# The last attention tile of a two-layer patch transformer: banks, projections and masked keys in another order

## The chip, the cores and the metric

One core of a Trainium2 chip runs the whole program. The metric is the device time of one execution in microseconds, the median of several runs. Engines are TensorE (PE in the profile, PEld for its weight loads), VectorE (DVE), ScalarE (ACT), GpSimd (POOL) and SyncE (SP, which only issues transfers here). All numbers are float32. PSUM, into which TensorE writes, has eight banks, numbered 0 to 7.

## The reference, cut to what matters

64 images give 49 patch tokens each, 3,136 rows of 192. There are two layers, each with a norm behind the residual:

```python
h = tok(x)                                   # (64, 49, 192)
h = layernorm(h + attention(h))              # causal, 12 heads of 16, relative positions
h = layernorm(h + attention2(h))             # qkv = h @ Wqkv.T + bqkv + routed low-rank delta
# attention2: softmax(q k^T * 0.25) v, then out @ Wproj.T + bproj
```

The change touches the end of the second layer alone: scores, softmax, weighting of the values, out-projection, residual and norm of the last tokens.

## The kernel before

The work is cut in two ways. **Tiles** of two images (98 tokens, `T`) carry the attention: 32 tiles in each layer. **Blocks** of 128 tokens carry the projections and norms: 25 blocks, 0 to 24, the last of 64 tokens. A hand-written order (`CHAINS`) gives each attention tile a slot; slots 0 to 63 hold the 64 tiles, `LAST` is 63, and the loops of every engine run over the slots to `SLOTS` = 67. Lists such as `OUT2` (out-projection of the second layer) and `QKV2` say in which slot a block is served. Each engine has its own program, and semaphores order them; an engine takes its instructions strictly as written.

In a slot n the steps are these. TensorE transposes the probabilities of the tile of slot n-1 (`transpose_probs`, L592, twice three transposes into banks 2 and 3), multiplies them with its values (`weigh_values`, L605, into bank 2) and computes the scores of slot n+1 (`scores`, L555, banks 0 and 1, but 4 and 5 for the last tile, whose scores come one slot early, in slot 62). VectorE finds the maximum, subtracts it, and behind the exponent sums, inverts and scales. ScalarE takes the exponent, copies the transposed probabilities to SBUF (`take_pt`, L824) and copies the weighted values y (`take_y`, L831). The wait on `yt_ready` at the head of `transpose_probs` keeps bank 2 until y of the tile before is out.

Scores need masked keys, a block-diagonal copy of k that GpSimd makes (`block_diagonal`, L420, L434). Weighting needs block-diagonal values (`vbd`), placed by small transfers on SyncE's queue (`place_values`, L379, L385) once the block's value rows are in SBUF (`take_v`, L822). A transfer of an output block (L398) goes on the same queue.

A finished block goes through `out_project` (L618, matmuls L623 and L624, bank 6), `add_residual` (L995, reads bank 6), `ln_stats`, `ln_aggregate`, `inverse_deviation` on ScalarE (L858) and `normalise` on GpSimd (L440: a shift, L445, and a scaling, L448). Its residual buffers are two, the output buffers `o_sb` three.

Near the end `keep_busy` (L661) issues matmuls of the identity into bank 7 whose result nobody reads: 21 calls in slots 63 to 66 (5, then 3, in slot 63; 2, 4 and 3 in slot 64; 2 in each of 65 and 66). Each call of one float32 matmul appears as two MATMUL rows.

The last five blocks, 20 to 24, are projected in slots 61, 63, 64, 65 and 66. Tile 31 (the last, slot 63) lies in blocks 23 and 24. In slot 61 GpSimd does the norm of block 19 first and then the masked keys of the last tile.

Of the kernel before, what the change touches and what calls it, by code (L numbers as in the profile page):

```python
# [30 lines left out]
RING = 6 * T  # L31
LEAD = 8
XS = 5
OS = 3
VR = 6
VB = 4
SCALE = 0.25
# [107 lines left out]
routers = by_slot(ROUTED)  # L145
qkv2s = by_slot(QKV2)

OUT2 = [n + 2 + (n + 2 in [m + 2 for m in DONE1] + [len(CHAINS) - 2]) for n in DONE2]
out2 = by_slot(OUT2)
norm2 = by_slot([n + (n < len(CHAINS)) for n in OUT2])  # L150

# [21 lines left out]
def score_bank(n):  # L173

    return 4 if n == LAST else 0


def moves(t):
# [33 lines left out]
def build(nc, x, tok_w, w1a_in, w1b_in, add1_in, const_in, p1_in, lora_in, w2_in, b2_in, p2_in, out):  # L212
    with ExitStack() as ctx:
# [40 lines left out]
        class Layer:  # L254
            def __init__(self, n):
                if n == 1:
                    self.q, self.k, self.mask, self.scale = qk1[0:64], qk1[64:128], kmask[64:128], SCALE
                else:
                    self.q = sb(f"q{n}", [64, 3, RING])
                    self.k = sb(f"k{n}", [64, 3, RING])  # L260
                    self.mask, self.scale = kmask[0:64], 1.0
                self.kbd = [sb(f"kbd{n}_{u}", [64, 2, 3, T]) for u in range(2)]
                self.vrow = [sb(f"vrow{n}_{u}", [128, E]) for u in range(VR)]
                self.vbd = [sb(f"vbd{n}_{u}", [PP, 2, E]) for u in range(VB)]
                self.res = [sb(f"res{n}_{u}", [128, E]) for u in range(2)]
                self.st = sb(f"st{n}", [128, 6])
                self.pad = sb(f"pad{n}", [1, 1])
                self.mv = sb(f"mv{n}", [128, BLOCKS, 2])
                self.lnv = sb(f"lnv{n}", [128, BLOCKS])
                self.rstd = sb(f"rstd{n}", [128, BLOCKS])  # L270
                self.shift = sb(f"shift{n}", [128, BLOCKS])
                self.qk_done = sem(f"qk_done{n}")
                self.qk_ready = sem(f"qk_ready{n}")
                self.kbd_ready = sem(f"kbd_ready{n}")
                self.v_done = sem(f"v_done{n}")
                self.v_rows = sem(f"v_rows{n}")
                self.v_ready = [sem(f"v_ready{n}_{u}") for u in range(VB)]
# [126 lines left out]
        def _(pool):  # L404
# [35 lines left out]
            def normalise(L, b, to):  # L440
                nonlocal upper
                k = tokens(b)
                pool.wait_ge(*moved_k)
                pool.wait_ge(L.rstd_ready, b + 1)
                nc.gpsimd.tensor_scalar(L.shift[0:k, b:b + 1], L.mv[0:k, b, 0:1], L.rstd[0:k, b:b + 1], -1.0,  # L445
                                        ALU.mult, ALU.mult).then_inc(L.shift_ready, 1)
                pool.wait_ge(L.shift_ready, b + 1)
                nc.gpsimd.tensor_scalar(to, L.res[b % 2][0:k], L.rstd[0:k, b:b + 1], L.shift[0:k, b:b + 1],  # L448
                                        ALU.mult, ALU.add).then_inc(L.ln_ready, 1)
                upper = L.ln_ready, b + 1  # L450

# [14 lines left out]
                    bias_values(b)  # L466
            for n in range(SLOTS):

                layer, t = attention(n + 2)
                known = bool(layer and (QKV1 if layer == 1 else QKV2)[block_of(t)] < n)  # L470
                if known:
                    block_diagonal(n + 2)
                for b in out1(n):
                    normalise(L1, b, h[0:tokens(b), b, :])
                for b in norm2(n):
                    if b >= OS:
                        pool.wait_ge(out_stored[b % OS], 16 * (b // OS))
                    normalise(L2, b, o_sb[b % OS][0:tokens(b)])
                if not known:
                    block_diagonal(n + 2)  # L480
                for b in turns(n):
                    bias_values(b)

        @block.tensor
        def _(pe):
# [104 lines left out]

            def transpose_probs(n, free):
                pf = probs[n % 2][:].rearrange("p h j -> p (h j)")  # L592
                if n > 0:
                    pe.wait_ge(yt_ready, n)
                if free:
                    pe.wait_ge(*free)
# [1 line left out]
                for half in range(2):  # L598
                    for g in range(3):
                        k = (3 * half + g) * 128  # L600
                        last = nc.tensor.transpose(ps[0:PP, 2 + half, g * PP:(g + 1) * PP], pf[:, k:k + PP],  # L601
                                                   ident[0:PP, 0:PP])
                    last.then_inc(ptr_done[half], 1)

            def weigh_values(L, t, n):  # L605
                pe.wait_ge(L.v_ready[t % VB], moved(t))
                values = L.vbd[t % VB][:].rearrange("p s (u c g) -> p s u c g", u=3, g=2)
                for half in range(2):
                    pe.wait_ge(pt_ready[half], n + 1)
                    for s in range(2):  # L610
                        for g in range(3):
                            last = nc.tensor.matmul(  # L612
                                ps[32 * g:32 * g + 32, 2, half * T + s * S:half * T + (s + 1) * S],
                                values[:, s, (3 * half + g) // 2, :, (3 * half + g) % 2],
                                pt[n % 2][:, 3 * half + g, s * PB:s * PB + S], start=True, stop=True)
                last.then_inc(pv_done, 1)

            def out_project(L, w, b, slot_of, free):  # L618
# [4 lines left out]
                nc.tensor.matmul(ps[0:k, 6, 0:E], yt[0:C, 1, lo:lo + k], w[0:C, 1, :], start=True, stop=False)  # L623
                nc.tensor.matmul(ps[0:k, 6, 0:E], yt[:, 0, lo:lo + k], w[:, 0, :], start=False, stop=True  # L624
                                 ).then_inc(L.proj_done, 1)
                return L.res_ready, b + 1

# [32 lines left out]

            def keep_busy(count):  # L661

                pe.wait_ge(L2.v_rows, BLOCKS)
                for _ in range(count):
                    nc.tensor.matmul(ps[:, 7, 0:128], ident, ident, start=True, stop=True)

            bank3 = bank4 = bank5 = bank6 = None

            for n in range(FIRST, SLOTS):
                before, u = attention(n - 1)  # L670
# [6 lines left out]
                if not bare:  # L677
                    for b in out2(n):
                        if b == 0:
                            pe.wait_ge(p2_loaded, 16)  # L680
                        if n > LAST:
                            keep_busy(2)
                        bank6 = out_project(L2, p2, b, SLOT2, bank6)

                split = bool(n <= 1 and turns(n))
                if split:
# [7 lines left out]
                if before:  # L694
                    if n == 1:
                        pe.wait_ge(zeros_ready, 2)
                    if n == LAST:
                        keep_busy(5)
                    if n == LAST + 1:
                        keep_busy(4)  # L700
                    transpose_probs(n - 1, bank3)
                    if n >= LAST:
                        keep_busy(3)
                    if n == LAST - 1:
                        scores(L2, attention(LAST)[1], LAST)
# [33 lines left out]
                    weigh_values(L1, u, n - 1)  # L739
                if before == 2:  # L740
                    weigh_values(L2, u, n - 1)
                if bare:
                    for b in out2(n):
                        if b == 0:
                            pe.wait_ge(p2_loaded, 16)
                        if n > LAST:
                            keep_busy(2)
# [16 lines left out]
        def _(act):  # L764
# [59 lines left out]
            def take_pt(n):  # L824
                if n >= 2:
                    act.wait_ge(pv_done, n - 1)
                for half in range(2):
                    act.wait_ge(ptr_done[half], n + 1)
                    nc.scalar.copy(pt[n % 2][:, 3 * half:3 * half + 3, :].rearrange("p g i -> p (g i)"),  # L829
                                   ps[0:PP, 2 + half, 0:3 * PP]).then_inc(pt_ready[half], 1)  # L830

            def take_y(n, t):
                act.wait_ge(pv_done, n + 1)
                nc.scalar.copy(yt[0:C, :, T * t:T * t + T],
                               ps[0:C, 2, 0:2 * T].rearrange("p (c t) -> p c t", c=2)).then_inc(yt_ready, 1)

            def take_h1(b, bank):
                k, lo = tokens(b), first_token(b)
# [28 lines left out]
            for n in range(FIRST, SLOTS):  # L867
# [18 lines left out]
                    exponent(n)  # L886
                if before and copies_late:
                    take_pt(n - 1)
                for b in norm2(n):
                    inverse_deviation(L2, b)  # L890
                for b in qkv2s(n):
                    if not urgent(b):
# [17 lines left out]
                        inverse_deviation(L1, b)  # L910
                if before:
                    take_y(n - 1, u)
                if n == LAST - 1:
                    exponent(LAST)
                if not turns(n) and not embeds(n):
# [11 lines left out]
        def _(dve):  # L927
# [67 lines left out]
            def add_residual(L, b):  # L995
                k = tokens(b)
                dve.wait_ge(L.proj_done, b + 1)
                if b >= 2:
                    dve.wait_ge(L.ln_ready, b - 1)
                nc.vector.tensor_tensor(L.res[b % 2][0:k], ps[0:k, 6, 0:E], h[0:k, b, :], ALU.add  # L1000
                                        ).then_inc(L.res_ready, 1)

            def ln_stats(L, b):
                k = tokens(b)
                dve.wait_ge(L.res_ready, b + 1)
                nc.vector.bn_stats(L.st[0:k], L.res[b % 2][0:k]).then_inc(L.st_ready, 1)

            def ln_aggregate(L, b):
                k = tokens(b)
# [33 lines left out]
            for n in range(FIRST, SLOTS):  # L1043
# [8 lines left out]
                    subtract(LAST)  # L1052
                for b in out1(n):
                    add_residual(L1, b)
                if n != LAST:
                    for b in out2(n):
                        add_residual(L2, b)
                for b in out1(n):
# [5 lines left out]
                if layer:  # L1064
                    sum_probs(n)
                    invert_sums(n)
                    scale_probs(n)
                if n == LAST:
                    for b in out2(n):
                        add_residual(L2, b)  # L1070
                for b in out2(n):
                    ln_stats(L2, b)
                for b in out2(n):
                    ln_aggregate(L2, b)
                for b in turns(n):
                    take_qk1(b)
# [82 lines left out]
```

## Time and profile before

| | |
|---|---|
| median of 3 runs | 389.62 us (389.46 to 390.89) |
| the profiled execution | 389.8 us |
| its span | 388.0 us |
| TensorE busy | 373.9 us, 96% |
| VectorE busy | 303.0 us, 78% |
| ScalarE busy | 215.9 us, 56% |
| GpSimd busy | 123.1 us, 32% |
| mean granted TensorE clock | 0.996 |

The span runs from the first to the last instruction that the profiler recorded. A busy share is an average over stages with different limits, and TensorE's holds the fillers of `keep_busy` too. All positions in the text are microseconds from the start of the span.

### The profile page before, as it was taken

To read this page: it belongs to the slowest core of one execution; us is meant where nothing else is said; L and a number is where in the kernel's file an instruction comes from. 1 tells how busy PE (TensorE), PEld (TensorE's weight loads), DVE (VectorE), ACT (ScalarE), POOL (GpSimd) and SP (SyncE) were. 2 spreads that over 40 slices of the span, in tenths; PEclk is the share of its full clock that TensorE was granted. 3 is DMA by queue.
4 is the path that set the end of the run, shared out by engine and by line. 5 is a ranking of instruction groups with operands and counts; after the bars stand their busy time and mean duration, and the time that the engine had idled before them with its cause. 6 is when DMAs were issued, how large, how long until landed. Compare 5 with 4: busy or idle time off the path is not lost.

```text
span 388.0 us, 13738 instructions
## 1 busy us (share of the span) xinstructions
PE 373.9 (96%) x5312; PEld 328.4 (85%) x5312; DVE 303.0 (78%) x814; ACT 215.9 (56%) x692; POOL 123.1 (32%) x262
## 2 busy tenths in 40 slices
PE   5999999999999999999999999999999999999994
PEld 4888788988889888988898888888898888877983
DVE  7368677678778877988878888788898888698882
ACT  1254565655546656465655666656665575655642
POOL 1222422321234424131325223251425232424213
PEclk9999999999999999999999999999999999999998
DMA  7742521221022112420032201111011101111111
GB/s 268 231 104 61 138 55 22 68 56 50 15 68 69 25 22 69 107 56 14 16 68 66 71 8 29 17 31 25 20 18 28 30 21 18 17 27 24 26 34 39
DMA packets 49338, 20.68 MB, mean 53 GB/s; under 512 B 41262, under 2 KB 45713, under 8 KB 49274
## 3 DMA queue, kind: packets, MB, share of 16 engines
q1 hardware_dynamic: 45530, 10.43, 12.7%
q10 hardware_dynamic: 3744, 9.38, 8.1%
q8 instruction: 43, 0.70, 0.8%
q14 instruction: 21, 0.17, 0.1%
HBM read 12.57 MB, written 2.41 MB: 39 GB/s over the span
## 4 chain that ended last, share of the span: by engine, by line
PE 87%; DVE 4%; ACT 3%; issue 3%; POOL 2%; DMA 1%; POOLq 0%; ACTq 0%
PE ps L496 13%; PE ps L601 10%; PE ps L574 10%; PE ps L612 7%; PE ps L586 6%; PE ps L623 5%; PE ps L550 4%; PE ps L548 4%; PE ps L546 4%; PE ps L624 4%; PE ps L526 3%; PE ps L532 3%; PE ps L530 2%; PE ps L568 2%; PE ps L634 2%
## 5 line engine op out<-in xcount | busy, mean ns | idle before, releaser
L958 DVE TENSOR_REDUCE mx<-ps 113x12 f32<-113x588 f32 x64 | 48.8, 763 | 25.4 <-PE ps L574 25.0
L984 DVE TENSOR_REDUCE psum<-probs 113x12 f32<-113x588 f32 x64 | 48.5, 757 | 21.2 <-ACT probs L815 21.1
L496 PE MATMUL ps<-tokw,xs 128*128 128x192 f32 (+1 forms) x300 | 57.0, 339 | 4.6 <-DMA tokw<-in_tokw 4.6
L815 ACT ACTIVATE probs<-probs 113x588 f32<-113x588 f32 x64 | 45.4, 709 | 27.0 <-DVE probs L965 26.2
L829 ACT COPY pt<-ps 113x339 f32<-113x339 f32 x128 | 49.4, 438 | 19.2 <-PE ps L601 19.1
L445 POOL TENSOR_SCALAR shift<-mv,rstd 128x1 f32<-128x1 f32 (+1 forms) x50 | 14.3, 286 | 140.7 <-ACT rstd L864 140.7
L434 POOL TENSOR_SCALAR kbd<-k,const 64x294 f32<-64x294 f32 x64 | 34.4, 547 | 74.2 <-ACT q L808 68.4
L496 PEld LDWEIGHTS ps<-tokw,xs 128*128 128x128 f32 (+1 forms) x300 | 49.7, 195 | 7.1 <-DMA xs<-in_x 4.2
L993 DVE TENSOR_TENSOR probs<-probs,rsum 113x588 f32<-113x588 f32 x64 | 50.8, 794 | 2.2
L601 PE MATMUL ps<-const,probs 113*113 113x113 f32 x384 | 50.1, 266 | 1.6 <-DVE probs L993 1.0
L965 DVE TENSOR_TENSOR probs<-ps,mx 113x588 f32<-113x588 f32 x64 | 49.4, 771 | 2.2
L601 PEld LDWEIGHTS ps<-const,probs 113*113 113x113 f32 x384 | 44.7, 178 | 6.0 <-issue 4.2
L434 POOL TENSOR_SCALAR kbd<-qk,const 64x294 f32<-64x294 f32 x64 | 32.5, 520 | 31.3 <-DVE qk L978 27.7
L612 PEld LDWEIGHTS ps<-pt,vbd 113*32 113x32 f32 x1536 | 26.6, 110 | 12.3 <-issue 9.6
L612 PE MATMUL ps<-pt,vbd 113*32 113x49 f32 x1536 | 35.3, 210 | 0.3 <-ACT pt L829 0.2
L802 ACT COPY k<-ps 64x384 f32<-64x384 f32 (+11 forms) x30 | 12.0, 417 | 33.6 <-PE ps L550 33.6
L546 PE MATMUL ps<-h1t,w 96*128 96x128 f32 (+1 forms) x150 | 29.0, 274 | 0.0
L548 PE MATMUL ps<-h1t,w 105*128 105x128 f32 (+1 forms) x150 | 29.0, 274 | 0.0
L550 PE MATMUL ps<-hwt,b 128*128 128x128 f32 (+1 forms) x150 | 29.0, 274 | 0.0
L623 PE MATMUL ps<-p,yt 96*128 96x192 f32 (+1 forms) x100 | 27.1, 352 | 0.0
L574 PE MATMUL ps<-kbd,q 32*49 32x98 f32 x768 | 23.2, 248 | 1.3 <-POOL kbd L434 1.3
L624 PE MATMUL ps<-p,yt 97*128 97x192 f32 (+1 forms) x100 | 24.5, 325 | 0.0
(93 smaller groups left out, 781.5 us busy)
## 6 DMA issues: line engine op xcount, KB each, us to landing
xs<-in_x ACTq DMA_DIRECT2D x22, 384.0 KB, 3.9
vbd<-vrow SPq DMA_DIRECT2D x160, 18.4 KB
out<-o SPq DMA_DIRECT2D x24, 96.0 KB, 1.8
xs<-in_x SPq DMA_DIRECT2D x2, 384.0 KB, 6.9
tokw<-in_tokw ACTq DMA_DIRECT2D x3, 192.0 KB, 3.7
w<-in_w SPq DMA_DIRECT2D x1, 472.5 KB, 4.4
xs<-in_x SPq DMA_DIRECT2D x3, 128.0 KB, 3.4
add<-in_add SPq DMA_DIRECT2D x1, 361.5 KB, 7.7
```

The lines of the kernel that those rows point to most:

```text
L434: last = nc.gpsimd.tensor_scalar(L.kbd[t % 2][:, e], L.k[:, :, at:at + T], L.mask[:, e:e + 1], L.scale, ALU.mult, ALU.mult)
L496: last = nc.tensor.matmul(ps[0:k, bank, 0:E], xs[:, b % XS, m, 0:k], tokw[:, m, :], start=(m == 0), stop=(m == KX - 1))
L574: last = nc.tensor.matmul(ps[s * PB:s * PB + S, score_bank(n) + half, m * T:(m + 1) * T], L.q[32 * half:32 * half + 32, m, at + s * S:at + ...
L601: last = nc.tensor.transpose(ps[0:PP, 2 + half, g * PP:(g + 1) * PP], pf[:, k:k + PP], ident[0:PP, 0:PP])
L612: last = nc.tensor.matmul(ps[32 * g:32 * g + 32, 2, half * T + s * S:half * T + (s + 1) * S], values[:, s, (3 * half + g) // 2, :, (3 * ha ...
L623: nc.tensor.matmul(ps[0:k, 6, 0:E], yt[0:C, 1, lo:lo + k], w[0:C, 1, :], start=True, stop=False)
L815: nc.scalar.activation(p, p, ACT.Exp).then_inc(exp_ready, 1)
L829: nc.scalar.copy(pt[n % 2][:, 3 * half:3 * half + 3, :].rearrange("p g i -> p (g i)"), ps[0:PP, 2 + half, 0:3 * PP]).then_inc(pt_ready[hal ...
L958: nc.vector.tensor_reduce(mx[n % 2][:].rearrange("p (b h) -> p b h", b=2), score_view(n), AX.X, ALU.max).then_inc(mx_ready, 1)
L965: nc.vector.tensor_tensor(probs_view(n), score_view(n), spread(mx[n % 2]), ALU.subtract).then_inc(sub_ready, 1)
L984: nc.vector.tensor_reduce(psum[:].rearrange("p (b h) -> p b h", b=2), probs_view(n), AX.X, ALU.add).then_inc(sum_ready, 1)
L993: nc.vector.tensor_tensor(probs_view(n), probs_view(n), spread(rsum), ALU.mult).then_inc(p_ready, 1)
```

## The change

- **Order of the out-projections.** `OUT2` of every block that would be served in slot 61 or later (`LATE2`, blocks 20 to 24) becomes at least slot 63. Block 20 moves from slot 61 to 63, where 21 already is; 22, 23 and 24 stay in 64, 65 and 66. All other blocks keep their slot.
- **Two banks.** Blocks 20, 22 and 24 use bank 6, blocks 21 and 23 use bank 7 (`out2_bank`).
- **The last transposes.** Those of slot 63's tile, and its weighting, go to banks 0 and 1 (`turned_bank`). They wait for the subtraction of slot 62 in place of y of slot 62, and are issued at the end of slot 63, directly behind the weighting of slot 62, and so ahead of block 22's projection.
- **Fillers.** 7 calls in place of 21: 2 ahead of slot 62's transposes and 3 behind them, and 2 ahead of block 23's projection. They write bank 4 and wait for the last subtraction.
- **VectorE and ScalarE.** From slot 63 on, residual, statistics and aggregate of a block follow each other, behind the last scaling. Of the norms of one slot ScalarE does the first where it did them all, and the others behind the copy of y.
- **The last masked keys.** In slot 61 GpSimd makes them ahead of the norm of block 19.
- **Buffers.** Second layer's residual buffers go from 2 to 4, output buffers from 3 to 5.

```diff
-OS = 3
+OS = 5
...
-OUT2 = [n + 2 + (n + 2 in [m + 2 for m in DONE1] + [len(CHAINS) - 2]) for n in DONE2]
+OUT2 = [n + 2 + (n + 2 in [m + 2 for m in DONE1]) for n in DONE2]
+
+LATE2 = [b for b in range(BLOCKS) if OUT2[b] >= len(CHAINS) - 3]
+for b in LATE2:
+    OUT2[b] = max(OUT2[b], len(CHAINS) - 1)
...
+def turned_bank(n):
+
+    return 0 if n == LAST else 2
+
+
+def out2_bank(b):
+
+    return 7 if b in LATE2 and (b - LATE2[0]) % 2 else 6
...
-                self.res = [sb(f"res{n}_{u}", [128, E]) for u in range(2)]
+                self.res = [sb(f"res{n}_{u}", [128, E]) for u in range(2 * n)]
...
-                known = bool(layer and (QKV1 if layer == 1 else QKV2)[block_of(t)] < n)
+                known = bool(layer and (QKV1 if layer == 1 else QKV2)[block_of(t)] < n) or n + 2 == LAST
...
-                if n > 0:
+                if n == LAST:
+                    pe.wait_ge(sub_ready, n)
+                elif n > 0:
                     pe.wait_ge(yt_ready, n)
...
-                pe.wait_ge(L2.v_rows, BLOCKS)
+                pe.wait_ge(sub_ready, LAST + 1)
                 for _ in range(count):
-                    nc.tensor.matmul(ps[:, 7, 0:128], ident, ident, start=True, stop=True)
+                    nc.tensor.matmul(ps[:, 4, 0:128], ident, ident, start=True, stop=True)
...
-                        if n > LAST:
+                        if n == LAST + 2:
                             keep_busy(2)
-                        bank6 = out_project(L2, p2, b, SLOT2, bank6)
+                        if out2_bank(b) == 6:
+                            bank6 = out_project(L2, p2, b, SLOT2, bank6)
+                        else:
+                            bank7 = out_project(L2, p2, b, SLOT2, bank7, 7)
...
                     if n == LAST:
-                        keep_busy(5)
-                    if n == LAST + 1:
-                        keep_busy(4)
-                    transpose_probs(n - 1, bank3)
-                    if n >= LAST:
+                        keep_busy(2)
+                    if n <= LAST:
+                        transpose_probs(n - 1, bank3)
+                    if n == LAST:
                         keep_busy(3)
...
                 if before == 2:
                     weigh_values(L2, u, n - 1)
+                if n == LAST:
+                    transpose_probs(LAST, None)
...
-                for b in norm2(n):
+                for b in norm2(n)[:1]:
                     inverse_deviation(L2, b)
...
                     take_y(n - 1, u)
+                for b in norm2(n)[1:]:
+                    inverse_deviation(L2, b)
...
-                if b >= 2:
-                    dve.wait_ge(L.ln_ready, b - 1)
+                if b >= len(L.res):
+                    dve.wait_ge(L.ln_ready, b - len(L.res) + 1)
...
-                if n != LAST:
+                if n < LAST:
                     for b in out2(n):
                         add_residual(L2, b)
...
-                if n == LAST:
-                    for b in out2(n):
+                for b in out2(n):
+                    if n >= LAST:
                         add_residual(L2, b)
-                for b in out2(n):
                     ln_stats(L2, b)
-                for b in out2(n):
                     ln_aggregate(L2, b)
```

## Rows read from the trace of the kernel before

**Rows 1.** The page of the profiled execution: span and instructions.
```profile
span 388.0 us, 13738 instructions
```
**Rows 2.** Chain that ended last, 350 to 388: start us, us, what.
```profile
369.90 0.72 PE ps L574 x24
...
373.07 1.12 PE ps L665 x10
...
379.70 0.48 PE ps L612 x24
...
381.69 0.45 PE ps L665 x4
...
382.14 0.54 PE ps L623 x2
...
382.68 0.34 PE ps L624 x2
...
383.04 0.36 DVE res L1000
```
**Rows 3.** Timeline, 363 to 370: start us, us, engine, line, op, out<-in.
```profile
367.07 0.20 ACT L864 ACTIVATE rstd<-lnv 128x1 f32<-128x1 f32 x1
...
367.46 0.72 POOL L445 TENSOR_SCALAR shift<-mv,rstd 128x1 f32<-128x1 f32 x1 [2.47 <-ACT rstd L864]
...
367.46 0.32 ACT L802 COPY k<-ps 64x192 f32<-64x192 f32 x1 [0.20 <-PE ps L550]
...
367.79 0.32 ACT L808 ACTIVATE q<-ps 64x192 f32<-64x192 f32 x1
...
368.02 0.30 ACT L834 COPY yt<-ps 96x196 f32<-96x196 f32 x1
...
368.49 0.85 PE L601 MATMUL ps<-const,probs 113*113 113x113 f32 x6
...
368.75 1.00 POOL L434 TENSOR_SCALAR kbd<-k,const 64x294 f32<-64x294 f32 x2
```
**Rows 4.** Timeline, 371 to 383, same columns.
```profile
371.78 0.31 ACT L822 COPY vrow<-ps 64x192 f32<-64x192 f32 x1 [0.43 <-PE ps L586]
...
374.97 0.77 DVE L993 TENSOR_TENSOR probs<-probs,rsum 113x588 f32<-113x588 f32 x1
...
378.81 0.79 ACT L829 COPY pt<-ps 113x339 f32<-113x339 f32 x2 [2.32 <-PE ps L601]
...
379.63 0.55 PE L612 MATMUL ps<-pt,vbd 113*32 113x49 f32 x24
...
380.35 0.30 ACT L834 COPY yt<-ps 96x196 f32<-96x196 f32 x1
...
381.73 0.36 DVE L1000 TENSOR_TENSOR res<-ps,h 128x192 f32<-128x192 f32 x1 [3.18 <-PE ps L624]
...
382.52 0.18 DVE L1012 BATCH_NORM_AGGREGATE mv<-st 128x2 f32<-128x6 f32 x1
```
**Rows 5.** Timeline of the SyncE queue: two closing and then six value transfers issued.
```profile
345.12 1.73 SPq L385 DMA_DIRECT2D vbd<-vrow  x2
...
372.12 4.89 SPq L385 DMA_DIRECT2D vbd<-vrow  x6
```
**Rows 6.** Windows, one slice: us, busy of each engine, PEclk, DMA share, GB/s.
```profile
347.50:347.75 0.25, 0.25 (x4) 0.25 (x4) 0.21 (x2) 0.00 (x0) 0.25 (x2) 1.00 0.47 72
```
**Rows 7.** The output tensor's transfers from 360 on: issue to landing.
```profile
DMA to landing us min/median/max: 1.6/1.8/3.9
```
**Rows 8.** Windows at the end, columns as in rows 6.
```profile
383.00:385.00 2.00, 0.00 (x1) 0.00 (x0) 0.87 (x4) 0.73 (x4) 1.01 (x3) 0.98 0.06 18
...
385.00:388.00 3.00, 0.00 (x0) 0.00 (x0) 0.00 (x0) 0.00 (x0) 0.49 (x2) 0.50 0.16 49
```
**Rows 9.** Groups by line: embedding matmuls to 9.4 us, then over the page.
```profile
L496 PE MATMUL ps<-tokw,xs 128*128 128x192 f32 x14 | 5.1, 542 | 4.6 <-DMA tokw<-in_tokw 4.6
...
L496 PE MATMUL ps<-tokw,xs 128*128 128x192 f32 (+1 forms) x300 | 57.0, 339 | 4.6 <-DMA tokw<-in_tokw 4.6
```

More of the change, by code:

```diff
@@ L447, in normalise @@
                 pool.wait_ge(L.shift_ready, b + 1)
-                nc.gpsimd.tensor_scalar(to, L.res[b % 2][0:k], L.rstd[0:k, b:b + 1], L.shift[0:k, b:b + 1],
+                nc.gpsimd.tensor_scalar(to, L.res[b % len(L.res)][0:k], L.rstd[0:k, b:b + 1], L.shift[0:k, b:b + 1],
                                         ALU.mult, ALU.add).then_inc(L.ln_ready, 1)
@@ L600, in transpose_probs @@
                         k = (3 * half + g) * 128
-                        last = nc.tensor.transpose(ps[0:PP, 2 + half, g * PP:(g + 1) * PP], pf[:, k:k + PP],
+                        last = nc.tensor.transpose(ps[0:PP, turned_bank(n) + half, g * PP:(g + 1) * PP], pf[:, k:k + PP],
                                                    ident[0:PP, 0:PP])
@@ L612, in weigh_values @@
                             last = nc.tensor.matmul(
-                                ps[32 * g:32 * g + 32, 2, half * T + s * S:half * T + (s + 1) * S],
+                                ps[32 * g:32 * g + 32, turned_bank(n), half * T + s * S:half * T + (s + 1) * S],
                                 values[:, s, (3 * half + g) // 2, :, (3 * half + g) % 2],
@@ L616, in weigh_values, with out_project @@
                 last.then_inc(pv_done, 1)
-            def out_project(L, w, b, slot_of, free):
+            def out_project(L, w, b, slot_of, free, bank=6):
                 k, lo = tokens(b), first_token(b)
@@ L622, in out_project @@
                 pe.wait_ge(yt_ready, slot_of[last_tile(b)] + 1)
-                nc.tensor.matmul(ps[0:k, 6, 0:E], yt[0:C, 1, lo:lo + k], w[0:C, 1, :], start=True, stop=False)
-                nc.tensor.matmul(ps[0:k, 6, 0:E], yt[:, 0, lo:lo + k], w[:, 0, :], start=False, stop=True
+                nc.tensor.matmul(ps[0:k, bank, 0:E], yt[0:C, 1, lo:lo + k], w[0:C, 1, :], start=True, stop=False)
+                nc.tensor.matmul(ps[0:k, bank, 0:E], yt[:, 0, lo:lo + k], w[:, 0, :], start=False, stop=True
                                  ).then_inc(L.proj_done, 1)
@@ L661, in keep_busy @@
             def keep_busy(count):
-                pe.wait_ge(L2.v_rows, BLOCKS)
+                pe.wait_ge(sub_ready, LAST + 1)
                 for _ in range(count):
-                    nc.tensor.matmul(ps[:, 7, 0:128], ident, ident, start=True, stop=True)
+                    nc.tensor.matmul(ps[:, 4, 0:128], ident, ident, start=True, stop=True)
             bank3 = bank4 = bank5 = bank6 = None
+            bank7 = L2.v_rows, BLOCKS
             for n in range(FIRST, SLOTS):
@@ L745, in _ @@
                             pe.wait_ge(p2_loaded, 16)
-                        if n > LAST:
-                            keep_busy(2)
                         bank6 = out_project(L2, p2, b, SLOT2, bank6)
@@ L829, in take_pt @@
                     nc.scalar.copy(pt[n % 2][:, 3 * half:3 * half + 3, :].rearrange("p g i -> p (g i)"),
-                                   ps[0:PP, 2 + half, 0:3 * PP]).then_inc(pt_ready[half], 1)
+                                   ps[0:PP, turned_bank(n) + half, 0:3 * PP]).then_inc(pt_ready[half], 1)
             def take_y(n, t):
@@ L834, in take_y @@
                 nc.scalar.copy(yt[0:C, :, T * t:T * t + T],
-                               ps[0:C, 2, 0:2 * T].rearrange("p (c t) -> p c t", c=2)).then_inc(yt_ready, 1)
+                               ps[0:C, turned_bank(n), 0:2 * T].rearrange("p (c t) -> p c t", c=2)).then_inc(yt_ready, 1)
             def take_h1(b, bank):
@@ L997, in add_residual @@
                 dve.wait_ge(L.proj_done, b + 1)
-                if b >= 2:
-                    dve.wait_ge(L.ln_ready, b - 1)
-                nc.vector.tensor_tensor(L.res[b % 2][0:k], ps[0:k, 6, 0:E], h[0:k, b, :], ALU.add
+                if b >= len(L.res):
+                    dve.wait_ge(L.ln_ready, b - len(L.res) + 1)
+                bank = out2_bank(b) if L is L2 else 6
+                nc.vector.tensor_tensor(L.res[b % len(L.res)][0:k], ps[0:k, bank, 0:E], h[0:k, b, :], ALU.add
                                         ).then_inc(L.res_ready, 1)
@@ L1005, in ln_stats @@
                 dve.wait_ge(L.res_ready, b + 1)
-                nc.vector.bn_stats(L.st[0:k], L.res[b % 2][0:k]).then_inc(L.st_ready, 1)
+                nc.vector.bn_stats(L.st[0:k], L.res[b % len(L.res)][0:k]).then_inc(L.st_ready, 1)
             def ln_aggregate(L, b):
```

## Prediction

> **What bounds the kernel now.** I read the page first, then the chain of waits over its last 40 us, then the timeline of the same stretch, the queue of SyncE, and last the windows with the granted clock. The profiled execution took 389.8 us, of which the span is 388.0 [rows 1] and 1.8 us lie around it. It is 0.2 us above the median of the three runs, 389.62. The difference that I work out below is taken off the median.
>
> The edits act only from slot 61 on (five output blocks, 20 to 24, and the tile of slot 63, the last). In the slots before that the same instructions run in the same order, with two more buffers in each of two rings. No row shows a wait for either ring, so I cost the buffers at nothing, and everything up to 366 us stays. In the chain [rows 2] the reader is to see that TensorE runs from 369.90 to 383.02 without an entry of another engine, and that this includes fillers (L665): 21 calls of keep_busy, 42 matmuls, of which the chain gives 10 one piece of 1.12 us. A filler ahead of a wait is not work, so "TensorE is the bound" is only the appearance. I therefore looked for what each real step waits for. The last tile's probabilities are scaled at 375.74 (374.97 + 0.77) [rows 4]; its weighting starts at 379.63 [rows 4]. These 3.9 us are what the change can reach. They pass because the last tile's transposes go through bank 2, which holds the tile before until its y has been copied, and because one out-projection and six fillers stand ahead of them.
>
> **Step 1, the masked keys ahead of the norm.** Now GpSimd does the shift of norm 19 at 367.46 (0.72 us), then its scaling, and starts the last masked keys at 368.75; they end at 369.75 and the last scores start 0.15 later, at 369.90 [rows 2, 3]. The keys need q of block 24, copied until 368.11 [rows 3]. After the change GpSimd waits for q alone. Does q come earlier? TensorE drops an out-projection (block 20) in slot 61, 0.54 + 0.34 = 0.88 us [rows 2], but ScalarE is busy with the norm until 367.27; from there k and q take 0.32 each, with 0.03 between, so q ends at about 367.95, 0.16 sooner [rows 3]. Keys then run about 368.05 to 369.05, and the last scores could start at 369.2, 0.7 earlier. TensorE must be there: the transposes of slot 62 (0.85 us) need y, which ScalarE copies in 0.30 behind q, until 368.27, in place of 368.32 [rows 3]. So they run 368.3 to 369.15, just ahead of the keys. If they stay at 368.49 the gain is 0.55; if q does not move it is 0.55 too. I take 0.7, with 0.5 and 0.8 as the ends. Queued behind the keys on GpSimd is now norm 19, ready only about 370.0; its store goes on SyncE's queue ahead of the value transfers of the last tile, whose rows are not there until 371.4. It holds nobody up.
>
> **Step 2, what the 0.7 carries.** Scores, block 24's value projection, the weighting of slot 61, both exponents and both scalings follow in the same order, so all move by 0.7: the value rows are ready at 371.39 in place of 372.09, the last scaling ends at 375.05 [rows 4]. Two out-projections (20 and 21) then stand where one stood: 1.75 us for 0.88. Fillers ahead of the transposes go from five calls (1.12) to two (0.45). The transposes of slot 63 start now at 373.07 + 1.12 = 374.19, and then at 374.19 - 0.7 + 0.88 - 0.67 = 373.7 [rows 2]. The extra projection so costs 0.2 of the 0.7 on this branch.
>
> **Step 3, the last transposes in banks 0 and 1.** They no longer wait for y of the tile before and go directly behind its weighting. I sum without overlap: transposes 0.85 [rows 3], copies 0.79 [rows 4], weighting 0.48 [rows 2] from 373.7 give 375.8; transposes and copies once more, 1.64, give 377.45. With the copies overlapping the transposes it is some 0.4 earlier for each tile, 376.7. Removed ahead of it: the out-projection of block 22, which goes behind the transposes and is done by 377.3, and 2 + 4 + 3 filler calls. If that were all, the last weighting would start between 376.7 and 377.5, 2.1 to 2.9 earlier than 379.63.
>
> **Step 4, what is late next: the value rows.** The last tile's block-diagonal values come in six small transfers on SyncE's queue, 372.12 to 377.01 (4.89 us, 0.82 each) [rows 5], issued as soon as block 24's rows are there. The profile gives no landing for them, so I bound it. The two that close an earlier tile are issued until 346.85, and traffic goes on until the slice that ends at 347.75, 0.9 later [rows 5, 6]. The output stores, the nearest transfers with a landing, take 1.6 to 3.9 us, median 1.8, from issue [rows 7]; less the 0.82 of the issue that is 0.8, 1.0 and 3.1 after its end. I take 1.2 (the traffic and 0.3 for the signal); ends 0.9 and 3.1. Now it lands near 378.2 and is hidden, 1.4 us ahead of 379.63. Moved by 0.7 the queue is done at 376.3 and the values land at 377.5, so this, rather than the copies, should release the last weighting, at 377.6: 2.0 us sooner than now. TensorE will idle about half a microsecond ahead of it. The cover of this transfer is gone; each tenth that it is later costs a tenth.
>
> **Step 5, the two banks behind it.** From the weighting to the y copy (380.35, 0.30) [rows 4] and the out-projection of block 23, nothing changes, two filler calls included. Block 24's projection starts now at 382.14, behind fillers (381.69, 0.45) and the residual of block 23, which reads the same bank [rows 2, 4]. In bank 6 it follows directly: 0.45 saved. But VectorE still has residual, statistics and aggregate of block 23 (381.73 to 382.70, 0.97) [rows 4], and its projection ended only at 381.69. TensorE is done 0.88 behind it; the residual of block 24 must then wait about 0.13 more for VectorE. Net 0.3. From 383.04 to the end, 4.96 us [rows 1, 2], all is the same chain for a 64-row block. The norms of 20, 21 and 22 pile up ahead: norm 20 runs in the wait, 21 and 22 behind y, some 0.85 us of GpSimd each (a shift and a scaling); they end near 381, before norm 23. I cost them at nothing; if they are in the way, one, 0.85, is the price.
>
> **Sum.** 2.0 + 0.3 = 2.3 us, a span of 385.7, and 387.3 by the median. That is 0.6%, close to the 0.5% (1.95 us) that a measurement of this kernel can tell from no change.
>
> **The clock.** TensorE stays at the full level (2.4 GHz) until its work is over: granted clock 0.98 in 383 to 385, 0.50 after it, while its last matmul ended at 383.02 [rows 2, 8]. So it outlasted nearly two microseconds without a matmul. The change cuts the fillers from 21 calls to 7 and opens idle spots of 0.2, 0.4 and 0.6 us, all shorter than that stretch. What the lower level costs: the embedding matmul takes 542 ns in the first 9.4 us, 339 over the kernel [rows 9], 1.6 times. The Trainium skill, "TensorE: Matmul & The Clock Gate", section "What's actually happening", says that the default is the throttled state and that activity releases it; by that rule filler removed is a risk, and no run here yet shows the lower level within the tail.
>
> **The rivals.**
> A, forecast: values release the last weighting, full clock; 386.6 to 387.7. Chance 0.60.
> B, the values are no limit (landing under 0.9, or the rows come earlier): the copies are, with the weighting at 376.7 to 377; 2.9 + 0.3 gives 386.4. For: nothing but the uncertain landing. 0.08.
> C, less comes through: step 1 gives 0.5, or the landing takes 2 in place of 1.2, or a norm stands in the way (0.85). Sum 1.1 to 1.9, 387.7 to 388.5. Nothing done at all by the new order, as the values are hidden anyway now, would need the landing at 3 or more. 0.17.
> D, the clock falls in the idle spot before the last weighting. Weighting 0.48 and two projections 1.76 run 1.6 to 2 times as long, 1.3 to 2.2 more: 388.7 to 389.5. Against: rows 8. 0.08.
> E, the other side: the clock falls once the fillers of slot 63 are gone, by about 372. From there to the end of the projections stand some 8 us of TensorE work, of which 0.8 fits in its idle time: 0.6 x 8 - 0.8 = 4.0 more at 1.6 times and 7.2 at double, so 391.3 to 394.5. It decides if the fall comes before about 374; later it is D. Against: that stretch has real matmuls in place of the fillers. 0.07.
>
> **The numbers.** Faster by over 0.5%: A and B, 0.68. Within: C and D, 0.25. Slower: E, 0.07. The range from 386.4 to 388.8 takes B, A, C and the near end of D, leaving out E and most of D.
>
> **What would show it.** Right: last scores near 369.2; six value transfers from 371.4; an idle spot of TensorE before the last weighting, which starts at 377.6, with the copies done by 377.4; the last two projections without a gap, ending near 380.6; clock 1.00 up to there. Wrong: a weighting directly behind the copies (B), scores later than 369.4, or a norm on GpSimd just ahead of norm 24's shift (C), matmuls of 1.6 times their length (D, E). What would make it wrong at the root is a difference ahead of 366 us, where I expect none.

## The result

The changed kernel took 386.52 us, the median of 8 runs (386.15 to 388.4); the kernel before took 389.5 beside it (8 runs, 389.02 to 391.62). The ratio is 0.9921, 95% interval 0.9898 to 0.9943: faster by 0.8%, where 387.3 and 0.6% were forecast. The page after answers to [rows 1]:

```profile
span 384.7 us, 13681 instructions
...
PE 369.7 (96%) x5284; PEld 324.3 (84%) x5284; DVE 303.1 (79%) x814; ACT 216.4 (56%) x692; POOL 122.5 (32%) x262
```

The spans differ by 3.3 us, but not all of it is the change. Up to slot 60 all engines run the same instructions, and I use the copies that ScalarE makes in slot 60 as a mark. This is the timeline before (start us, us, engine, line, operation):

```profile
7.45 2.86 PE L496 MATMUL ps<-tokw,xs 128*128 128x192 f32 x10 [0.37 <-DMA tokw<-in_tokw]
...
360.49 0.76 ACT L829 COPY pt<-ps 113x339 f32<-113x339 f32 x2
```

and this after:

```profile
7.45 1.98 PE L511 MATMUL ps<-tokw,xs 128*128 128x192 f32 x10 [0.40 <-DMA tokw<-in_tokw]
...
359.60 0.76 ACT L849 COPY pt<-ps 113x339 f32<-113x339 f32 x2
```

The second ten embedding matmuls took 0.88 us less in this execution, and at the mark the kernel is 0.89 ahead; in between nothing moves. I take the start as not the change's doing: no edit touches it, and in the fourteen profiles of this study the mark lies anywhere between 359.60 and 362.51. What speaks for this is weighed at the end of the account of the prediction. So I compare **the stretch from the mark to the end of the span**: 388.0 - 360.49 = 27.5 us before, 384.7 - 359.60 = 25.1 after. By this measure the change is worth 2.4 us; the other 0.9 of this pair is the start.

The chain that ended last, after, answers to [rows 2]:

```profile
368.40 0.72 PE ps L589 x24
...
370.28 0.32 ACT vrow L842
...
370.62 0.71 SPq L399
...
374.75 2.03 DMA vbd<-vrow
...
376.82 0.55 PE ps L629 x24
377.37 0.64 PE ps L682 x4
378.01 0.44 PE ps L640 x2
378.46 0.34 PE ps L641 x2
...
378.82 0.37 DVE res L1023
```

Where the chain before was TensorE alone, it now goes from the last scores over the value rows to SyncE's queue, and through a transfer into the last weighting. The timeline after, answering to [rows 3, 4, 5]:

```profile
366.84 0.32 ACT L828 ACTIVATE q<-ps 64x192 f32<-64x192 f32 x1
...
367.25 1.00 POOL L448 TENSOR_SCALAR kbd<-k,const 64x294 f32<-64x294 f32 x2 [3.15 <-ACT q L828]
...
368.23 0.26 POOL L459 TENSOR_SCALAR shift<-mv,rstd 128x1 f32<-128x1 f32 x1
...
370.62 4.89 SPq L399 DMA_DIRECT2D vbd<-vrow  x6
...
374.56 0.85 PE L618 MATMUL ps<-const,probs 113*113 113x113 f32 x6
...
375.20 0.79 ACT L849 COPY pt<-ps 113x339 f32<-113x339 f32 x2 [0.20 <-PE ps L618]
...
376.82 0.55 PE L629 MATMUL ps<-pt,vbd 113*32 113x49 f32 x24 [0.75 <-DMA vbd<-vrow]
...
377.43 0.32 ACT L854 COPY yt<-ps 96x196 f32<-96x196 f32 x1 [1.02 <-PE ps L629]
...
379.71 0.33 DVE L1023 TENSOR_TENSOR res<-ps,h 64x192 f32<-64x192 f32 x1
```

The reader is to see the bracket at 376.82: the copies were done at 375.99, and TensorE sat 0.75 us until the values had landed. From the mark, the last scores come 0.61 sooner than before (8.80 for 9.41), the last weighting 1.92 sooner (17.22 for 19.14), and the last residual 2.44 sooner (20.11 for 22.55).

### The profile page after: what moved, and what is told of

Read it like the earlier page. It is cut to its first block, busy times and chain, and to the rows that moved or that the text cites. A ratio compares the mean times of both kernels' runs of the same rounds, so it can differ in the third digit from the quotient of the medians.

```text
span 384.7 us, 13681 instructions
## 1 busy us (share of the span) xinstructions
PE 369.7 (96%) x5284; PEld 324.3 (84%) x5284; DVE 303.1 (79%) x814; ACT 216.4 (56%) x692; POOL 122.5 (32%) x262
## 4 chain that ended last, share of the span: by engine, by line
PE 86%; DVE 3%; ACT 3%; issue 3%; DMA 2%; POOL 1%; SPq 1%; POOLq 0%; ACTq 0%
PE ps L511 12%; PE ps L589 10%; PE ps L618 10%; PE ps L629 7%; PE ps L601 6%; PE ps L640 4%; PE ps L565 4%; PE ps L563 4%; PE ps L561 4%; PE ps L641 3%; PE ps L541 3%; PE ps L547 3%; PE ps L545 2%; PE ps L583 2%; PE ps L651 2%
## 5 line engine op out<-in xcount | busy, mean ns | idle before, releaser
L835 ACT ACTIVATE probs<-probs 113x588 f32<-113x588 f32 x64 | 45.3, 708 | 27.0 <-DVE probs L987 26.2
L511 PE MATMUL ps<-tokw,xs 128*128 128x192 f32 (+1 forms) x300 | 56.1, 336 | 4.6 <-DMA tokw<-in_tokw 4.6
L511 PEld LDWEIGHTS ps<-tokw,xs 128*128 128x128 f32 (+1 forms) x300 | 48.9, 192 | 7.0 <-DMA xs<-in_x 4.1
L629 PEld LDWEIGHTS ps<-pt,vbd 113*32 113x32 f32 x1536 | 26.6, 110 | 13.3 <-issue 9.6
L854 ACT COPY yt<-ps 96x196 f32<-96x196 f32 x64 | 20.2, 316 | 8.0 <-PE ps L629 7.5
```

The lines of the kernel that those rows point to most:

```text
L511: last = nc.tensor.matmul(ps[0:k, bank, 0:E], xs[:, b % XS, m, 0:k], tokw[:, m, :], start=(m == 0), stop=(m == KX - 1))
L629: last = nc.tensor.matmul(ps[32 * g:32 * g + 32, turned_bank(n), half * T + s * S:half * T + (s + 1) * S], values[:, s, (3 * half + g) // ...
L835: nc.scalar.activation(p, p, ACT.Exp).then_inc(exp_ready, 1)
```

## The experiments

Each kernel has the stretch from the mark to the end as its measure; repeated, the changed kernel gave it again to 0.02 us. "Median" is given for the kernels that ran six times or more; the others ran once, in the profiled execution.

| kernel | mark, span | stretch, us | median, us (before beside it) |
|---|---|---|---|
| before | 360.49, 388.0 | 27.5 | 389.5 |
| changed | 359.60, 384.7 | 25.1 | 386.52 |
| changed, again | 359.98, 385.1 | 25.1 | 386.91 (389.59) |
| 1 rows early | 360.60, 384.9 | 24.3 | 386.29 (389.25) |
| 2 two transfers more | 360.21, 388.8 | 28.6 | 390.24 (389.25) |
| 3 banks 2 and 3 | 360.17, 385.3 | 25.1 | 387.06 (389.25) |
| 4 no fillers | 359.60, 384.7 | 25.1 | 386.6 (389.25) |
| 5 keys behind norm | 360.47, 386.2 | 25.7 | |
| 6 one bank | 359.96, 389.3 | 29.3 | |
| 7 before, fewer fillers | 360.19, 386.8 | 26.6 | |
| 8 before, keys first | 362.51, 389.5 | 27.0 | |
| 9 rows early, no fillers | 360.42, 384.6 | 24.2 | 386.71 (389.59) |
| 10 transposes behind 22 | 360.01, 385.4 | 25.4 | |
| 11 transfers and fillers | 359.86, 386.7 | 26.8 | |

**1. Rows early.** Is it the values that the last weighting waits for? Of the six transfers two read block 23's rows, which are there long before.

```diff
 for t in tiles_from(n - 1, QKV2):
     place_values(L2, t, SLOT2)
+    if t == TILES - 2:
+        place_values(L2, TILES - 1, SLOT2, True)   # only the pieces of block 23; shortened
```

> The changed kernel, but the two value transfers of the last tile that read block 23's rows are issued behind those of the tile before, in SyncE's idle time, and only the four of block 24 wait for its rows. Measure: the stretch from the copies of slot 60's transposed probabilities to the end of the span, 27.5 us before the change and 25.1 behind it. Theory V (the landing of the values releases the last weighting): they land 1.2 us sooner, the weighting then waits for its copies, which ended 0.8 us ahead of it, and the stretch is 24.3. Rival T (TensorE's own order and its copies set the pace, the wait for the transfer is only where the profile puts it): 25.1, no change.

24.3 us, as theory V had it. In its timeline eight transfers run in one, the store of block 19 follows, and four wait for their turn behind it:

```profile
365.12 6.34 SPq L404 DMA_DIRECT2D vbd<-vrow  x8
371.50 0.47 SPq L419 DMA_DIRECT2D out<-o  x1
372.08 3.51 SPq L404 DMA_DIRECT2D vbd<-vrow  x4
...
376.18 0.79 ACT L856 COPY pt<-ps 113x339 f32<-113x339 f32 x2 [0.20 <-PE ps L625]
...
376.56 0.49 PE L648 MATMUL ps<-p,yt 97*128 97x192 f32 x2
...
376.98 0.41 PEld L636 LDWEIGHTS ps<-pt,vbd 113*32 113x32 f32 x24 [0.22 <-DMA vbd<-vrow]
376.98 0.55 PE L636 MATMUL ps<-pt,vbd 113*32 113x49 f32 x24
```

T falls: moving the values moves the end. But the forecast has two errors that hide each other. The values did not come 1.2 us sooner. The store of block 19 now stands between the two early transfers and the four late ones, which start 11.48 us behind the mark in place of 11.02, so the queue ends at 375.59, 0.92 sooner than in the changed kernel. Of these 0.92 the weighting got 0.84 (16.38 us behind the mark for 17.22). And the copies are not the new limit, although they end at 376.97, just ahead of the weighting. The code needs only the first half of them to start the weighting, and that is done at about 376.6. TensorE goes from block 22's projection (L648) to the weighting without an idle time of its own, and the one wait left is that of the weight load, 0.22 us for the transfer. With a landing 1.27 us behind the queue, as measured in the changed kernel, the values would be there at 376.86, so values and TensorE's own order lie within about 0.1 us of each other; which of them comes last the trace does not separate.

**2 and 11. Two transfers more, and fillers in the wait.**

```diff
+if L is L2 and t == TILES - 1:
+    for e in range(2):   # 49 rows each into a spare buffer
+        sp.dma_start(spare[...], L.vrow[...]).then_inc(spare_done, 16)
 for b, row, s, at, k in moves(t):
```

> The changed kernel with two transfers more, of 49 rows each into a spare buffer that nobody reads, ahead of the last tile's six on SyncE's queue; nothing else waits for them but the end. Theory V: each holds the queue 0.82 us, all of it passes on, stretch 25.1 + 1.6 = 26.7 us. Rival T: at least the 0.8 us between copies and weighting is slack, so 25.1 to 25.9.

28.6, not 26.7. The weighting started 1.8 us later (1.6 expected: the queue ended 1.6 later, and the last transfer took 2.19 us in place of 2.03), and 1.7 more followed. The timeline and the windows (us, busy of each engine, PEclk, DMA share, GB/s) of kernel 2:

```profile
379.21 0.62 PE L636 MATMUL ps<-pt,vbd 113*32 113x49 f32 x24 [2.54 <-DMA vbd<-vrow]
379.76 1.22 PE L689 MATMUL ps<-const 128*128 128x128 f32 x4
380.77 0.85 PE L647 MATMUL ps<-p,yt 96*128 96x192 f32 x2
```

```profile
377.00:379.00 2.00, 0.00 (x0) 0.00 (x0) 0.60 (x4) 0.01 (x1) 0.76 (x2) 1.00 0.16 32
379.00:381.00 2.00, 1.79 (x29) 1.68 (x30) 0.00 (x0) 1.06 (x5) 0.19 (x1) 0.64 0.12 40
381.00:383.00 2.00, 2.00 (x7) 1.38 (x7) 0.67 (x2) 0.04 (x1) 1.31 (x4) 0.50 0.15 49
```

TensorE had no matmul for 2.54 us, the granted clock fell from its upper level (2.4 GHz) to the lower (1.2) just behind, and the matmul pair of an out-projection took 0.85 where it takes 0.56 in kernel 11 below. Kernel 11 puts fillers into that wait:

```diff
 if before == 2:
+    if n == LAST + 1:
+        keep_busy(10)
     weigh_values(L2, u, n - 1)
```

> The kernel with two transfers more and, in TensorE's wait of 2.5 us ahead of the last weighting, 10 filler calls. In the run with two transfers alone the stretch was 28.6 in place of 26.7, and the granted clock fell 0.35 us behind the start of the weighting. Theory K (the extra 1.7 us is the lower clock, brought on by the longer wait): the clock stays at its full level and the stretch is 26.9. Rival W (the extra is another wait, a queue behind the two transfers): 28.6 again.

26.8, the clock at its upper level in the windows of the same place:

```profile
376.00:378.00 2.00, 2.00 (x19) 2.00 (x19) 1.09 (x7) 0.63 (x3) 0.76 (x2) 1.00 0.10 16
378.00:380.00 2.00, 1.70 (x34) 1.40 (x33) 0.00 (x0) 0.51 (x2) 0.00 (x0) 1.00 0.21 59
380.00:382.00 2.00, 1.61 (x9) 0.99 (x8) 1.07 (x5) 0.73 (x4) 1.39 (x4) 1.00 0.00 0
```

In both kernels the weighting starts 19.0 us behind the mark. So two transfers cost 1.7 us by themselves (26.8 against 25.1) and 1.8 through the clock. Both halves of theory K hold and W falls. The clock did not fall this far in every execution of kernel 2: ten of the twelve have a mean granted clock of 0.986 to 0.991 and 389.58 to 392.96 us, the other two 0.997 and the shortest times, 388.8 and 389.04. The rule of the Trainium skill weighed in the prediction ("TensorE: Matmul & The Clock Gate", "What's actually happening": activity releases the throttle) agrees with this trace.

**3. Banks 2 and 3.** `turned_bank` returns 2 for every slot, and the last transposes wait for y of slot 62.

> The changed kernel, but the last tile's transposes and weighting use banks 2 and 3 again and wait for y of the tile before; their place in the order stays. Theory V: they start about 0.5 us later (y is copied at 375.0, they started at 374.56), their copies end at 376.5, still ahead of the landing at 376.8, so the stretch stays at 25.1 us: the banks themselves gain nothing, the order does. Rival B (the other banks are where the gain is): 25.5 us or more, towards 27.

25.1. The transposes start 0.5 later and their copies end 0.3 ahead of the weighting. The banks of the title gain nothing here. The two late bank choices must be told apart: this one is free, that of experiment 6 is not.

**4. No fillers.** All three calls of `keep_busy` are gone.

> The changed kernel without the 7 filler calls that are left. Theory V: fillers stand ahead of waits and hide nothing; the clock stays at its full level to the last projection, stretch 25.1 us, at most 0.2 less. Rival K (the clock falls when they are gone): the last weighting and two projections take 1.6 to 2 times as long, 1.3 to 2.2 us more, 26.4 to 27.3, and the granted clock shows the lower level ahead of 379.

25.1. The windows of kernel 4, with TensorE busy 1.09 and 1.48 us of 2:

```profile
375.00:377.00 2.00, 1.09 (x19) 0.79 (x20) 1.75 (x9) 1.18 (x4) 0.47 (x2) 1.00 0.14 23
377.00:379.00 2.00, 1.48 (x30) 1.12 (x23) 0.19 (x1) 1.10 (x5) 0.83 (x3) 1.00 0.15 49
```

The granted clock stays at 1.00; K falls for this place.

**5. Keys behind the norm.** The `or n + 2 == LAST` is taken out of `known`.

> The changed kernel, but in slot 61 GpSimd does norm 19 ahead of the last masked keys, as before. Same measure: 25.1 us in the changed kernel. Theory V: keys, scores, value rows and values all move back by the 0.6 us that the new order brought (GpSimd then does shift and scaling first, which ended at 368.78 in the kernel before), stretch 25.7. Rival T (the pace is set by TensorE's tail order, not by the values): less than 0.2 of it reaches the end.

25.7: 0.6 of it in, 0.6 out. The value queue carries it whole.

**6. One bank.** `out2_bank` returns 6.

> The changed kernel with all the late out-projections in bank 6. Theory V: nothing until the last weighting; block 24's projection then waits for the residual of block 23, ends about 0.4 us later, and 0.1 of it was a wait for VectorE anyway, so the stretch is 25.4 us. Rival N (VectorE's and GpSimd's norms of 20 to 23 set the end, projections do not): 25.1.

29.3, far outside both. Theory V was wrong about what the second bank is for. The timeline and windows of kernel 6:

```profile
371.43 0.49 PE L641 MATMUL ps<-p,yt 97*128 97x192 f32 x2
374.91 0.59 PE L640 MATMUL ps<-p,yt 96*128 96x192 f32 x2 [2.99 <-DVE res L1023]
...
376.32 1.35 PE L618 MATMUL ps<-const,probs 113*113 113x113 f32 x6
```

```profile
375.00:377.00 2.00, 2.00 (x12) 2.00 (x13) 1.32 (x7) 0.00 (x0) 0.00 (x0) 0.72 0.12 19
377.00:379.00 2.00, 2.00 (x14) 1.77 (x15) 0.00 (x0) 0.88 (x2) 0.00 (x0) 0.50 0.01 4
```

In slot 63 two projections follow each other. The residual of block 20, which frees bank 6, now stands behind the last scaling on VectorE, at 374.50. Block 21 waits 2.99 us for it, the transposes of slot 62 with it, and the clock falls on top (0.72, then 0.50): they take 1.35 us for 0.82. How the 4.2 us split between wait and clock was not tried.

**7 and 8. Parts alone, on the kernel before.** Kernel 7 keeps 7 of the 21 filler calls; kernel 8 has the keys first.

> The kernel before with one part alone: of its 21 filler calls the 7 stay that the changed kernel has (2 and 3 in slot 63, 2 in slot 65), order, banks and keys untouched. Stretch 27.5 us before, 25.1 in the changed kernel. Theory V: the last transposes then follow block 22's projection directly, copies end at about 378.7 on the clock of the kernel before, the values land at 378.3, so the weighting starts 1.0 to 1.2 sooner than 379.63 and the last projection loses its filler too: stretch 26.2. Rival O (the new order of transposes is what gains): 27.3 or more.

> The kernel before with one part alone: the last masked keys ahead of norm 19 on GpSimd. Block 20's projection stays in slot 61. Theory V: q of block 24 comes at the same time, the keys 0.5 sooner, but TensorE still has 0.9 us more in slot 61, and its transposes end at 369.34, so the scores start at 369.35 in place of 369.90: stretch 27.0. Rival (the keys gain only together with the projection's move): 27.5.

Fewer fillers give 0.9 (26.6, between the 26.2 of V and the 27.3 of O, nearer V). The timeline around the last weighting:

```profile
377.63 0.79 ACT L827 COPY pt<-ps 113x339 f32<-113x339 f32 x2 [1.42 <-PE ps L601]
...
378.19 0.52 PEld L612 LDWEIGHTS ps<-pt,vbd 113*32 113x32 f32 x24 [0.53 <-DMA vbd<-vrow]
378.22 0.63 PE L612 MATMUL ps<-pt,vbd 113*32 113x49 f32 x24 [0.38 <-ACT pt L827]
...
379.06 0.20 ACT L862 ACTIVATE rstd<-lnv 128x1 f32<-128x1 f32 x1
379.17 0.30 ACT L832 COPY yt<-ps 96x196 f32<-96x196 f32 x1
```

The weighting now starts inside the last copies, and the profile names both for its wait: the transfer for the weight load, the copies for the matmul. It came 1.1 us sooner, as V had it; the missing 0.4 lies behind it. The copy of y stands on ScalarE directly behind two norms and starts 0.95 us after the weighting, where it was 0.72 before. And the filler that is gone ahead of the last projection gives nothing: from y to the last residual it is 2.69 us in both kernels, because that projection, at 380.95, waits 0.45 for the residual of block 23, which reads its bank. Keys first give 0.5 (27.0), as expected; the projection of block 20 need not move for it.

**10. Transposes behind block 22.** The call of `transpose_probs(LAST, ...)` goes back to slot 64.

> The changed kernel, but the last tile's transposes stand again in slot 64 behind block 22's out-projection, in banks 0 and 1. Theory V: block 22 waits for y of slot 62 (copied at 375.0) and takes 0.9, so transposes from about 376.0 and copies until 377.4, now 0.6 later than the values land: the copies take over as the limit, weighting at 377.45, stretch 25.7 us. Rival F (the gain came from the fillers alone): 25.1.

25.4, in the middle. Transposes start at 376.29, the weighting at 377.43, 0.2 later than in the changed kernel once the marks are set equal. I had summed whole copies; the weighting starts inside them, behind their first half (376.84 to 377.29).

**9, and the changed kernel again.** The early transfers without any filler.

> The changed kernel with the two early value transfers and without any filler. With early transfers the copies were the limit, 0.1 us behind the values, and without fillers the copies ended 0.16 sooner. Theory V: the landing (0.11 ahead of the copies' end before) becomes the limit again, stretch 24.27 less 0.1 to 0.2, so 24.1 us. Rival K (with nothing left to fill the waits the clock falls): 25.4 or more.

> The changed kernel as it is, beside the others on the same chip: stretch 25.1 us, and a median 2.4 us under that of the kernel before if only the tail differs; the 3.0 us seen first had 0.6 that no row of the tail explains.

24.2 and 25.1 us of stretch. In time, kernels 1, 9 and the changed one can't be told apart: ratios to the kernel before 0.9913 (0.9883 to 0.9942), 0.9919 (0.989 to 0.9947) and 0.9916 (0.9885 to 0.9947). Kernel 1 has the lowest median, 386.29, and its stretch says that 0.8 us are there; the spread of the start hides them. Kernel 9 gains 0.1 more, but the executions speak against it: two of its eleven took 390.18 and 393.58 us with a mean granted clock of 0.991 and 0.968, while kernel 1's six lie between 385.67 and 387.13 at 0.996 or more. That the missing fillers are the cause is not shown: kernel 4, also without them, had no such run in six. I would keep kernel 1. What kernel 9 was expected to show, copies and then values as the limit, its trace does not separate: the first half of the copies is done about 0.4 us ahead of the weighting, which follows block 22's projection directly.

## Why the prediction was right

The forecast was 2.3 us by rival A, with the values releasing the last weighting. Measured on the stretch, 2.4.

- **Step 1**, 0.7: the scores came 0.61 sooner. GpSimd started the keys 0.09 behind q. They ended at 368.25, but the scores started at 368.40, behind the transposes on TensorE (367.54 and 0.85). From the mark these had moved by 0.06 only, where the step took 0.2, so the gain is the 0.55 that the step gives for transposes that stay, and this 0.06. Experiments 5 and 8 give 0.6 and 0.5 for this part alone. The shift of the norm had taken 0.72 us at 367.46 [rows 3], beside VectorE's scaling of the probabilities (367.27 to 368.04); behind the keys, away from it, it takes 0.26. The Trainium skill ("SBUF — State Buffer", "Who interferes with whom") says that a VectorE instruction with two SBUF inputs contends with a GpSimd instruction that reads SBUF. The traces agree: in kernel 5, with the old order, the shift is beside the scaling and takes 0.72 again.
- **Step 2**, transposes of slot 62 at 373.7: 372.65 after, 373.54 on the clock of before.
- **Step 3**, copies done by 376.7 to 377.5: 375.99, 376.88 on that clock. Of the fillers taken away, 0.9 us is what they cost alone (experiment 7).
- **Step 4**, the landing 1.2 behind the end of the queue: the chain has 374.75 + 2.03 = 376.78, the queue ended at 375.51, so 1.27. The 1.2 was a choice near the lower of two bounds, 0.9 and 3.1, and no row carried its 0.3 for the signal; that it came out within 0.1 is in part luck. Weighting 1.92 sooner, 2.0 forecast. Experiments 1, 2, 5 and 11 move the values both ways and the end follows.
- **Step 5**, 0.3: measured 0.52, in two parts. y is copied 0.11 sooner behind the weighting, which I had at nothing: before, it stood on ScalarE directly behind a norm (380.24 and 0.20), and now it waits for TensorE alone. From y to the last residual it is 2.28 in place of 2.69. The step's picture of the second bank was too small. It was costed for block 24 alone, while its main work is block 21 in slot 63 (experiment 6). The residuals move behind the last scaling, and the step never asked who waits for their bank then.
- **Norms at nothing:** right to within 0.1. Norm 23's scaling ends at 381.41 on GpSimd and block 24's shift starts there.
- **The buffers at nothing** holds only for the kernel before. In the new order the residual of block 22 is taken at 376.11 and that of block 23 at 378.82, while GpSimd reads the residuals of 20 and 21 until 377.47 and 379.23. With two buffers both would have to wait, the second some 0.4 us on the way to the end. This is an estimate from the trace; no run keeps the two buffers.
- **The clock:** at its upper level to 383, so D and E did not happen. Experiment 2 shows that D is real once the wait is longer, at a price of 1.8 us; I had 1.3 to 2.2. The factor 1.6 for it came from a stretch in which the granted clock reads 1.00, so those rows do not show the lower level. The rows that do, in kernels 2 and 6, give 0.85 us for 0.56 and 1.35 for 0.82, 1.5 and 1.6 times.
- **The time itself** was 0.8 us under the forecast although the tail was right to 0.1. The rest lies ahead of 366 us, where the prediction expected nothing and called a difference a sign of being wrong at the root. The evidence is for scatter, not for a step of the prediction. The same changed kernel had 386.52 and 386.91, and its difference to the kernel before beside it was 3.0 and 2.7 us, where the stretch says 2.4 both times. The profiles alone don't settle it, since the kernel before and its variants 7 and 8 have three of the later marks (360.49, 360.19 and 362.51). The medians say more. Taking the 1.8 us around the span and the stretch off each gives the mark as an estimate: 360.2, 360.0 and 360.3 for the three series of the kernel before, and 359.6 to 360.7 for the changed kernel, twice, and kernels 1, 3, 4 and 9. So there is no lasting gain at the start. That 386.52 lies inside the range, 0.1 above its lower end, is in part luck: the range allowed nothing for this scatter.

Of the 2.4 us, experiment 8 gives 0.5 to the keys and experiment 7 gives 0.9 to the fillers, each alone; the last 1.0 is what the rest does on top of them, and was not split further. Moving the transposes ahead of block 22 is worth 0.3 (experiment 10), the banks 0 and 1 nothing (experiment 3).

## What to carry to other kernels

When a stretch of TensorE has no entry of another engine in the chain, look for fillers in it before calling TensorE the bound, and cost the transfer that becomes late once they are gone: here it took back 0.8 us that an earlier issue gave again. An earlier transfer pushes back what stands behind it on its queue, and copies in halves release their reader by the first half, so look at the wait itself before naming the new limit. When a reader of a PSUM bank is moved back in its engine's order, ask for each writer of that bank what it now waits for; the price may be the clock as well as the wait. Where the start of an execution scatters by more than the gain, measure from a mark behind it.

## What was not expected of the hardware

The time to the first blocks differs between executions of the same instructions. The embedding matmuls of kernel 8, the slowest start:

```profile
8.46 3.54 PE L496 MATMUL ps<-tokw,xs 128*128 128x192 f32 x10 [1.49 <-DMA tokw<-in_tokw]
```

Where the profiles show the same ten matmuls as one row, they took 1.86 to 3.54 us; those of kernel 8 began 1.0 later behind their weights, and its mark lies 2.9 us behind that of the changed kernel. The windows from 9 to 11 us, kernel 8 first, then the changed kernel (columns as above):

```profile
9.00:11.00 2.00, 2.00 (x8) 2.00 (x7) 1.04 (x2) 0.32 (x1) 0.29 (x1) 1.00 0.50 198
```

```profile
9.00:11.00 2.00, 2.00 (x16) 1.98 (x15) 1.04 (x2) 1.00 (x4) 0.08 (x1) 1.00 0.98 345
```

TensorE is busy all the time in both, with 8 matmuls in one and 16, mostly of the same shape, in the other, and the granted clock reads 1.00 in both. In slices of half a microsecond the pace goes from about 3 matmuls to 5 or more at some 8 us in the changed kernel, 9 in the kernel before, 10 in kernel 1 and 12 in kernel 8. So the start scatters by when TensorE leaves its slower pace, besides when its weights arrive; what sets that moment no run here shows. Several runs of the kernel before lie near 391.5 beside others near 389; a late start would explain them, but no profile of such a run was compared.
